# Redrawing the order of steps on all five engines of a macaron block, with TensorE's instruction packets counted

## What is computed

```
x = x + 0.5 * ffn(layernorm(x))        # run "1"
x = x + attn(layernorm(x))             # runs "A" (attention) and "L" (gated MLP)
x = x + 0.5 * ffn(layernorm(x))        # run "2"

ffn(x):  e = argmax(x @ gate_W.T + gate_b)            # one of 8 experts for each row
         relu(x @ wi.T + wi_b + lora_e(x)) @ wo.T + wo_b
attn(x): h = rmsnorm(x);  q, k, v, i, f from h        # 16 heads of width 16
         C_t = f_t C_(t-1) + i_t v_t k_t^T;  n_t = f_t n_(t-1) + i_t k_t
         y_t = C_t q_t / max(|n_t q_t|, 1);  x = x + y @ wo
         x + (silu(h2 @ w_gate) * (h2 @ w_up)) @ w_down,  h2 = rmsnorm(x)
```

## Time and profile before

| | before |
|---|---|
| median of three runs | 904.32 us |
| lowest and highest | 900.94 and 910.37 us |
| span of the profiled execution | 900.5 us |
| TensorE matmul busy | 844.4 us, 94% |
| VectorE / ScalarE / GpSimd busy | 622.3 / 359.0 / 249.6 us |
| DMA queue q8, instruction packets | 102 packets, 1.67 MB |

### The profile page before, as it was taken

How to read it: one execution, slowest core, us unless ns; L and a number is a source line. 1 busy time by engine, 2 the same in 40 slices (tenths; PEclk the granted TensorE clock), 3 DMA queues, 4 the chain that set the end, 5 groups by cost and what they waited for, 6 DMA issues and landing times.

```text
span 900.5 us, 30800 instructions
## 1 busy us (share of the span) xinstructions
PE 844.4 (94%) x12744; PEld 811.9 (90%) x12744; DVE 622.3 (69%) x1502; ACT 359.0 (40%) x716; POOL 249.6 (28%) x234
## 2 busy tenths in 40 slices
PE   3958899999899999999899999999999989999998
PEld 3958889999899998999799998899989979899998
DVE  6546795685857777576777868668585898697642
ACT  5453262434425353343523436244452462234421
POOL 2022343130442133221223224313044133612100
PEclk9989999999999999999999999999999999999999
DMA  9214535102434023402324302621043145510000
GB/s 249 84 35 119 158 98 161 54 26 61 116 116 109 13 64 100 131 27 65 85 77 134 96 24 70 176 80 53 9 116 114 42 126 134 158 47 2 1 25 24
DMA packets 66313, 76.04 MB, mean 84 GB/s; under 512 B 12702, under 2 KB 48670, under 8 KB 66176
## 3 DMA queue, kind: packets, MB, share of 16 engines
q1 hardware_dynamic: 66176, 74.09, 29.5%
HBM read 56.75 MB, written 17.30 MB: 82 GB/s over the span
## 4 chain that ended last, share of the span: by engine, by line
PE 77%; issue 6%; DVE 6%; SPq 4%; ACT 2%; POOL 2%; DMA 2%; ACTq 0%; POOLq 0%; DVEq 0%
PE bank L1092 22%; PE bank L1094 20%; PE bank L1093 20%; PE bank L1127 3%; SPq L437 3%; PE bank L1250 2%; PE bank L1310 2%; PE bank L1289 1%; PE bank L1329 1%; PE bank L1264 1%; PE bank L1344 1%; DMA parts_scratch<-pc 1%; DMA dm<-f_scratch 1%; PE bank L1270 1%; POOL pc L555 1%
## 5 line engine op out<-in xcount | busy, mean ns | idle before, releaser
L643 ACT ACTIVATE r_h<-bank 128x512 fp32r<-128x512 f32 x128 | 76.5, 598 | 232.1 <-PE bank L1127 175.3
L1092 PE MATMUL bank<-xT_hi,wi_hi 128*128 128x256 f32 x512 | 146.6, 286 | 1.7 <-DVE r_l L835 1.2
L1092 PE MATMUL bank<-wo_hi,r_h 128*128 128x256 f32 x512 | 146.2, 286 | 0.2
L1094 PE MATMUL bank<-xT_lo,wi_hi 128*128 128x256 f32 x512 | 143.7, 281 | 0.0
L1094 PE MATMUL bank<-wo_lo,r_h 128*128 128x256 f32 x512 | 143.7, 281 | 0.0
L1093 PE MATMUL bank<-wo_hi,r_l 128*128 128x256 f32 x512 | 143.7, 281 | 0.0
L1093 PE MATMUL bank<-xT_hi,wi_lo 128*128 128x256 f32 x512 | 143.5, 280 | 0.0
L835 DVE SCALAR_TENSOR_TENSOR r_l<-bank,r_h 128x512 fp32r<-128x512 f32 x128 | 87.6, 685 | 75.9 <-ACT r_h L643 75.7
L1092 PE MATMUL bank<-xT_hi,wgu_hi 128*128 128x256 f32 x352 | 101.7, 289 | 0.0
L1092 PEld LDWEIGHTS bank<-xT_hi,wi_hi 128*128 128x128 f32 x512 | 96.8, 189 | 3.6 <-DVE vq L915 1.7
L1094 PE MATMUL bank<-xT_lo,wgu_hi 128*128 128x256 f32 x352 | 98.3, 279 | 0.0
(11 more groups left out here) (157 smaller groups left out, 2114.2 us busy)
## 6 DMA issues: line engine op xcount, KB each, us to landing
dm<-f_scratch SPq DMA_DIRECT2D x128, 128.0 KB, 2.9
arena<-parts_scratch SPq DMA_DIRECT2D x96, 128.0 KB
arena<-parts_scratch SPq DMA_DIRECT2D x96, 64.0 KB
arena<-parts_scratch SPq DMA_DIRECT2D x32, 192.0 KB
x<-in_x SPq DMA_DIRECT2D x16, 256.0 KB, 3.1
parts_scratch<-pa SPq DMA_DIRECT2D x64, 64.0 KB
parts_scratch<-pb SPq DMA_DIRECT2D x64, 64.0 KB
parts_scratch<-pc SPq DMA_DIRECT2D x64, 64.0 KB
```

Source lines behind the costliest of these rows:

```text
L643: nc.scalar.activation(flat(r_h[:, n]), U[use % 2][:], ACT.Relu).then_inc(f_rh, 1)
L1092: nc.tensor.matmul(dst, lh, rh, start=first, stop=False, **more)
L1094: return nc.tensor.matmul(dst, lh, rl, start=False, stop=last, **more)
```

## The change

The five strings of `ORDER` are replaced by five others. The number of letters of each kind in each string is the same, so each stream's steps are the same and stand in the same order among themselves. What differs is where the steps of one stream stand between those of the others. No instruction, tile, wait or DMA is added or taken away. The diff shifts all line numbers by one, as the PE string has one line more.

```diff
 ORDER = {
     "PE": """
-        3G U G 5U 2V 4U 2V 4U 2V 2U 2V 2G 5U G U 2G 2U G 8U V U V 3U 2V 2U 2S Y U V 3U V U 2V 2M S M Y S Y G Y S M G 5U 2M U S Y U M G Y U S Y S M G M U M Y G
...
+        2G 2U 2G 4U 2V 2U V U V 4U V U V 2U 2V 2G 6U G U G U G U G 7U 2V 5U 2V U Y 2S 2U 2V 3U 2V 3M 2S Y S Y G M Y M G 5U S M U S Y M U G U Y M Y S G M U Y M
...
```

More of the change, by code:

```diff
@@ new lines @@
+        2U Y V 2U Y V Y S 2U 3M S V U Y U V Y 2U Y 2S G 2V 3M U Y U G Y U Y 2S 3U V 3M S V Y U Y V Y U 3M U Y U Y 2U 2V G V U G 5U 2V U G V 2U G 3U G V U G 2V
+        4U V U V G 3U V U G V 2U G U V G U V 3U V U V 4U V 2U 2V 2U V 3U V 2U V U 2V""",
+    "DVE": """
+        H 4G 2H G H 2G 2H G 2H R 4H 6R H R 2H R G H R 3G H 2G R G R 2G R G R 2H 2R G R H G H 2R H G R 2H G 4R H R H D 2R D 2R G 2P R 2D Y 2R Y D R 2G Y P G Y
+        P Y G Y D G R G R G R G D R P Y R G R Y P 2R Y P 2Y G R 2Y G 2R Y G 2R 2G Y R D R P Y 2R 3Y G D 2R Y 3G R D R G D R 3G R G R G 7R P R P G Y 2R Y R G
+        3R G 3R G P R 3G 3R G D Y 2R D G 2R Y R P G R D G R 3G 2R Y 2R Y D 2R Y R Y R P R P Y G Y P R Y G 2R G 2R G Y R Y R D Y G R P D Y R 2Y R G Y G R Y R
+        2G P R D R G 2R P 3R 2G R G R G R G R Y R D 3R Y G 3R G 2R G R Y R 3G 2R P R G D R G P R D R G R D G Y 2R 3G 3R G 2R Y D 2R Y R 2Y R G 2P R Y R Y G 2Y
+        2R G 2R G Y R D Y P R G Y P Y G Y R Y D R Y G Y 2G 4R G D P 3R G 5R P 2R Y 2G R 2G 3R D 2R G 2R Y G 2R G R D G 2R G R G P Y G R G 3R G Y 2D R P G R 2G
+        R G 2R G 2R Y R D R Y R P 2Y R G Y 2R Y G Y P Y R G 2R G R Y R D R Y D Y G R 2P Y G R G Y R Y R D Y R 2G R G R D 3R P 3R 3G R G 3R Y P G P 3R D 2R G R
+        G 3R G R 2G 2R G Y 2R Y G R P D G 3R Y G 2D 2R 2G Y G R G 2R G Y R P 3R 2Y P 2R Y G 2Y P Y G Y 2R G Y 2R G R D R G R G P Y R D 2Y D R 2Y 2R G Y 2G R D
+        R G P R P 5R G R G R 2G 2R G R D Y 2R Y R G 3R G 3R G R P G Y P 2R D 2G R G R D G R D 3R 3G Y R 2G R G 4R Y 2R Y R Y 2P Y R P Y G R Y R Y G Y R G 2R G
+        2R 2Y R 2D Y P R Y R G Y G Y R P R Y 3G R D P R G R 2D 4R G 2R 3G R Y 3R G D 6R P 3R G R P G Y 2R Y 2R G R Y 2G R Y R G 2Y P R Y D Y P G R D R Y G Y
+        2R G 2Y R G Y R P R D P G 3Y R D R 2Y D R P Y G Y G P 2G R Y R Y R 2D Y P R Y D P Y R D G R 2Y D Y R P R Y R Y 2R Y P 3R G Y G P R Y G D Y G P R Y 2R
+        Y R Y 2R Y 2G 4R G 2R G R G 3R 2G 3R G 3R G 4R G 2R G 2R 2G 2R 2G R G 2R 2G 2R G 2R G 12R""",
@@ L131 @@
-        E A E K 2E 3K 6A K 3A E F K F A E K E C K 2A 3E 2K E 2K 4O 2E 4O""",
+        H 7A F A E 2A F E K E K C A K E K X E A 2K 2E 2K 6A X A F E F A E A K A K C K 2E A K E A E K E 2K E K 8A F 3E F K A E 3K A C 2A 2O X K 2E 2K E K E 7A
+        F 2A 2E K F K O 2A 2E K O C A E X K 2E 3K E K 6A F E A F 2E K O C E 2A K A 2K O X E K A 2E A K E 2K 6A E A F A K 2E A E 2K F C O A K E A E O K X A E
+        3K E 7A E F K A E A K E K F K A C E K E A E A E K E K A K 5A E 2A F E O A K O K F E C K 2A K A 2E O E 2K E K E O K E 4O""",
```

50 lines of the change are left out of this document (18 added, 32 removed).

## The result

The changed kernel takes **923.71 us** (median of 4 runs, 921.92 to 924.82) against 905.48 us (4 runs, 900.94 to 910.37) for the kernel before: a ratio of 1.0202, 95% interval 1.0161 to 1.0242. The forecast was 902.5 us with a range of 893 to 911, and 0.1 for slower by over 1%. It was wrong. The run with the profile took 923.25 us for a span of 921.1 us, so some 2.1 us lie around the span, not the 0.4 us read off the lowest run before; the sum does not depend on it, as it carried over the distance of the median from the span as it was.

A forecast was written before the change was run, and what follows sets the result against it. TensorE was taken as the bound, so only its idle time (30.8 us in the first 110 us, 25.3 after) could change. -4.0 + 2.2 + 0 = -1.8 us from the median 904.3 gave 902.5 us, range 893 to 911.

The forecast's parts named there:

- Term 1, the packets: Five TensorE breaks at instruction-packet edges, 5.9 us: more work in the two packets before each wins 4.0 us.
- the count: Work in the two packets before each of five breaks, old against new order: 2.6 us go, 3.3 stay.
- Term 2, the start: Program start: two U steps ahead of the gate make the third U step later, at 26.4 to 28.1: +2.2 us.
- The order behind it to 80 us: TensorE's order after the start, to 80 us: a q step moves ahead of a wait, at no cost.
- Term 3, all other moves: Other moves on all engines and the DMA queue: work between waiting steps stays alike; 0 us, ends -8 and +8.
- Rival (c): An engine's list holds a step ahead of one TensorE needs sooner: +8 to +13 us, 910 to 915; chance 0.12.
- half of the 15.8 us of semaphore waits: Behind 110 us, this much TensorE waiting could be lost or added again: the ends of -8 and +8 us.

The follow-up runs named there:

- The shifted kernel: Kernel before with 26 tiny needless products (104 instructions) in the first idle time, so packet edges fall 104 instructions earlier: 918.4 us, ratio 1.0135.
- the q step alone: Kernel before with block 0's second q step ahead of the first transposes of block 1 in TensorE's list, nothing else moved: 904.7 us, ratio 1.0013.
- the splices: All engines' lists of the kernel before up to 103 or 275 us, then those of the changed kernel: 915.71 and 910.35 us.

## Why the prediction was wrong

- **Term 1, the packets: right in the sum, its rule only in part.** Read start to start, the breaks at packet edges were 6.9 us and are 2.2 (-4.0 forecast, -4.7 measured); on the page "issue" fell from 5.9 to under 1. All five old breaks are gone, also those at 339 and 742 us, which the count left nearly whole. The 2.2 us that remain stand at edges that the count did not name, at 113.6, 118.7, 369.3 and 802.1 us among them. More went than the count had and others came: that the two nearly cancel is luck. The shifted kernel shows that edges are where TensorE breaks, and also breaks behind pairs of packets that are not thin. The Trainium skill says in "Runtime: NRT & Kernel Launch", section "Instruction fetch mechanics", that refills are hidden. That does not hold here: breaks at edges last 6.9 us in the kernel before and 18.4 us in the shifted one.
- **Term 2, the start: its size right, its price too low.** The third U step starts at 27.45, inside 26.4 to 28.1, in part by luck: it begins 0.5 us later than I put it (14.74), both U steps run nearly to their end at the slow pace (one product every 0.21 us up to 19.58), and the way from the gate is shorter (7.53 us for 7.9 to 8.4). What is missing is the clock: the sum put +2.2 there and let all dense work behind run at the old pace. The bare chain brings half clock for 10.2 us and 2.3 to 2.7 us more. A row said it: the wide products of the earlier trace rows start every 0.23 us at 17.73 to 20.25 and every 0.125 from 21.32 on. I used both paces for the moved steps and did not ask what idle time does to the steps that did not move. The order behind it to 80 us, put at "nothing", cost another 2.6 us between 61.9 and 76.5 us of the kernel before. Which list does it was not taken apart: the q step alone sets the gate 1.0 us back, and with TensorE's own list as before the transposes of block 1 still wait.
- **Term 3, all other moves: the step that failed.** It was put at 0 with ends of 8 us. Behind 101 us of the kernel before, the changed kernel lost 12.4 us, although 4.7 were won at packet edges: some 17 us, twice the upper end. I counted the TensorE work between two ends of a chain and took that as its cover. Nothing was counted on the lists of VectorE, ScalarE and SyncE, where the chain itself has to stand in time. The places found (statistics ahead of `r_h` and of `r_l`, waiting for loads; splits of weights and a k step ahead of the choice) are of that kind, and TensorE's own list shows nothing of them. The clock is missing here as well.
- **Rival (c) is what happened,** with 0.12 and 910 to 915 us. Its mechanism is seen at three places. Its price of 0.5 to 0.8 us for a wait was that of one kind of wait in the old order; the new waits reach 2.9 us, and half clock behind one of them added some 2.3 us more.
- **The range** was too narrow: half of the 15.8 us of semaphore waits was a guess at what can be won, and the same figure was used for what can be added, which those waits do not bound.

In sum, of the 20.6 us of span, 11.5 are longer matmuls and 9.1 more idle time, in which 4.7 us fewer at packet edges hide 13.8 more of waits. Within the stretches of half clock (13.6 us before, 40.9 changed) TensorE is busy for 11.3 and 32.1 us. As a product of 256 columns starts every 0.21 us there and every 0.12 us elsewhere, I estimate from the 20.8 us between them that up to 9 of the 11.5 us are the clock; it is an upper end, as the clock costs nothing where another engine sets the pace.

**What stays open:** the 2.6 us behind block 1's gate and the 2.7 us between 732.9 and 784.8 us were not taken apart, nor was it tried to set the statistics of block 6 and their load right together. Between 444.8 and 463.9 us the changed order is 3.2 us ahead, 2.0 and 2.3 in the splices. A kernel as before with the changed lists there alone might win some 2 us by this; no such mixture was run, and whether the lists can be joined at both ends is not known.

## What to carry to other kernels

Where several engines work through fixed lists, a move has a price on each list: follow the chain to the wait and look what stands ahead of each of its steps on its own engine, first of all steps that wait for a DMA. Of a wait that you add before dense matmuls, count the clock of the work behind it, not only its length: it added 2.3 to 2.7 us at the start and some 2.3 behind a later wait. Compare two orders only at points where both have done the same work. And when instructions are added or taken away, read the edges of the instruction packets anew: 104 tiny ones cost 10 us here.

## What was not expected of the hardware

- The granted clock is at half for 40.9 us of the changed execution and 13.6 of that before. Near twins differ in it too: the kernel with one exchanged pair of steps had some 34 us of it in a profiled run that was the slowest of ten (910.6 us against a median of 904.7). One profile is good for a place, not for a total.
- Breaks at packet edges vary in the same way: edge 1729, near 110 us, has none in the kernel before and 2.1 us in the one with the exchanged pair.
- The clock column can read full where the pace is low. In the changed kernel it reads 1.00 for the window from 10 to 20 us, but wide products start every 0.21 us there up to 19.58 and every 0.12 or 0.13 behind it. The trace's first entry for the clock is at 19.6 us, so at the start of a program the pace, from start to start, is the safer reading.
